# First norm with the shift as dots on VectorE and chunks handed over singly; last block finished and stored chunk by chunk

## The reference

```python
mod = silu(c) @ ada_w.T + ada_b              # (B, 6 D)
shift_msa, scale_msa, gate_msa, shift_mlp, scale_mlp, gate_mlp = split(mod, 6)
h = rmsnorm(x, g1) * (1 + scale_msa) + shift_msa
q, k, v = heads(h @ qkv_w.T + qkv_b)         # q, k normed over 36, q scaled
o = softmax(q @ k.T) @ v                     # per head
x = x + tanh(gate_msa) * (o @ proj_w.T + proj_b)
h2 = rmsnorm(x, g2) * (1 + scale_mlp) + shift_mlp
x = x + tanh(gate_mlp) * (gelu(h2 @ fc1_w.T + fc1_b) @ fc2_w.T + fc2_b)
```

## Time and profile before

| | |
|---|---|
| median of 3 runs | 2960.52 us (2960.25 to 2960.9) |
| profiled execution, its own time | 2961.68 us |
| its span | 2959.8 us |
| TensorE (PE) busy | 98% |
| VectorE (DVE) busy | 67% |
| ScalarE (ACT) busy | 53% |
| GpSimd (POOL) busy | 7% |

### The profile page before, as it was taken

The page is one execution under the profiler, slowest core; times in us unless marked ns, Lnnn a source line. Parts: engine busy times, 40 slices in busy tenths (PEclk is TensorE's granted clock), DMA queues, the critical chain, the costliest instruction groups (busy, mean ns, idle before and its releaser), DMA issues.

```text
span 2959.8 us, 35431 instructions
## 1 busy us (share of the span) xinstructions
PE 2900.7 (98%) x13080; PEld 2194.8 (74%) x13080; DVE 1971.7 (67%) x2687; ACT 1581.8 (53%) x1926; POOL 220.1 (7%) x153
## 2 busy tenths in 40 slices
PE   8999996999999999999999999999999999999998
PEld 7999994666666666666666666688888888888886
DVE  5777775899888888888888887844343342424332
ACT  3333324677676676776776766634344343434342
POOL 3232301000000000000000000090000000000000
PEclk9999997999999999999999999999999999999999
DMA  5465545222222222322223223342222222322121
GB/s 211 150 194 160 177 142 157 63 82 76 75 83 76 74 72 75 86 77 79 79 62 86 73 76 95 116 139 89 72 85 72 80 77 91 102 77 88 41 68 45
DMA packets 238407, 282.85 MB, mean 96 GB/s; under 512 B 34912, under 2 KB 143968, under 8 KB 237344
## 3 DMA queue, kind: packets, MB, share of 16 engines
q1 hardware_dynamic: 232992, 270.18, 30.0%
q10 hardware_dynamic: 5248, 10.49, 1.0%
HBM read 195.66 MB, written 84.67 MB: 95 GB/s over the span
## 4 chain that ended last, share of the span: by engine, by line
PE 82%; DVE 1%; ACT 1%; SPq 0%; DMA 0%; issue 0%; POOL 0%; DVEq 0%; ACTq 0%; POOLq 0%
PE ps L1385 16%; PE ps L1410 16%; PE ps L1469 15%; PE ps L1452 15%; PE ps L1397 13%; PE ps L1428 4%; PE ps L1396 2%; ACT gated L1092 1%; DVE x L1267 0%; SPq L874 0%; DVE x L1271 0%; DVE x L1273 0%; DVE w_lo L1261 0%; DMA kT<-qk_hi_scratch 0%; POOL kT L1007 0%
## 5 line engine op out<-in xcount | busy, mean ns | idle before, releaser
L1039 ACT ACTIVATE p_r<-ps 128x1024 f32<-128x1024 f32 x512 | 491.9, 1024 | 423.6 <-PE ps L1385 423.6
L1216 DVE TENSOR_TENSOR p_lo<-p_r,p_hi 128x1024 fp32r<-128x1024 f32 x512 | 613.2, 1218 | 0.0
L1385 PE MATMUL ps<-qT,kT 110*128 110x512 f32 x2048 | 573.6, 397 | 21.2 <-DMA qT<-m_scratch 19.8
L1385 PEld LDWEIGHTS ps<-qT,kT 110*128 110x128 f32 x2048 | 382.8, 190 | 155.4 <-issue 51.4
L1039 ACT ACTIVATE prob<-ps 128x1024 f32<-128x1024 f32 x512 | 483.5, 1030 | 2.1 <-PE ps L1385 1.6
L1396 PE MATMUL ps<-prob,vp 128*64 128x512 f32 x1024 | 453.1, 595 | 0.0
L1397 PE MATMUL ps<-prob,vp 128*37 128x512 f32 x1024 | 451.7, 594 | 0.0
L1338 DVE TENSOR_TENSOR a_lo<-act,a_hi 128x512 fp32r<-128x512 f32 x144 | 102.7, 713 | 518.9 <-ACT a_hi L1082 518.9
L1210 DVE CAST p_hi<-p_r 128x1024 fp32r<-128x1024 f32 x512 | 350.1, 694 | 135.0 <-ACT p_r L1039 133.6
L1469 PE MATMUL ps<-a_hi,w 128*128 128x512 f32 x1296 | 415.6, 393 | 0.6 <-DVE a_lo L1338 0.6
L1410 PE MATMUL ps<-p_hi,vx 128*128 128x512 f32 x1024 | 404.1, 395 | 0.1
(11 more groups left out here) (165 smaller groups left out, 3612.5 us busy)
## 6 DMA issues: line engine op xcount, KB each, us to landing
w_raw<-w SPq DMA_DIRECT2D x144, 320.0 KB, 2.9
qk_hi_scratch<-aw SPq DMA_DIRECT2D x32, 576.0 KB, 3.1
qk_lo_scratch<-aw SPq DMA_DIRECT2D x32, 576.0 KB, 4.4
kT<-qk_hi_scratch SPq DMA_DIRECT2D x128, 144.0 KB
qT<-qk_hi_scratch SPq DMA_DIRECT2D x128, 144.0 KB
v_scratch<-stv SPq DMA_DIRECT2D x32, 512.0 KB, 2.6
vp<-v_scratch SPq DMA_DIRECT2D x16, 1024.0 KB, 9.1
xb<-xT SPq DMA_DIRECT2D x8, 1280.0 KB, 10.0
```

Of the source, the lines that this page charges most:

```text
L1039: act.activation(out, ps[:, 2 * slot:2 * slot + 2, :].rearrange("p a b -> p (a b)"), ACT.Exp).then_inc(exp_done, 1)
L1216: dve.tensor_tensor(p_lo[:, j], p_r[:, j], f32(p_hi[:, q % HIGHS]), ALU.subtract).then_inc(plo_done, 1)
L1385: mm = pe.matmul(ps[:, 2 * (entry % RING) + h, :], kT[r][:, h, kt * P:(kt + 1) * P], qT[:, u % 2, h], start=True, stop=True)
```

## The change

At the start: TensorE makes the scale alone, in one group; the shift of both sequences is made by dots on VectorE (`shift`), for sequence 0 ahead of the sum of squares, for sequence 1 after the first tile's weights are ready and ahead of the tile loop. The order of the weights `ada`, `adan` follows. The maximum and the product on 128x8 elements become tensor_tensor with a small tensor that is broadcast, prepared before. VectorE makes x * scale * norm in one operation per chunk (`scaled`), ScalarE adds the shift while it makes the high part, VectorE adds it again while it makes the low part (`h0_low`), and each low part releases one chunk of TensorE's first tile. The low parts of w, pieces 1, 2 and 3, are made in halves (chunks 0 and 1, chunks 2 to 4) and awaited so. Pieces 2 and 3 of w have buffers of their own and are loaded at once.

At the end: in block 7, TensorE finishes the partial chunk first at k = 17 and signals every chunk; gates and adds follow in that order; SP stores the partial chunk, chunks 0 and 1, chunk 2 and chunk 3 as four transfers.

```diff
+        w_raw2 = sb(st, "w_raw2", [P, KC, PIECE])
+        w_raw3 = sb(st, "w_raw3", [P, KC, PIECE])
...
+        W_HALVES = (slice(0, 2), slice(2, KC))
+        W_LOWS = ((0, slice(0, KC)),) + tuple((q, ks) for q in (1, 2) for ks in W_HALVES)
@@ SP
-                for s in range(2):
-                    sp.dma_start(aw01[:, s], ada[:, s]).then_inc(aw_ld[s], 16)
+                sp.dma_start(awp, ada).then_inc(aw_ld[1], 16)
+                sp.dma_start(aws, adan[0]).then_inc(aw_ld[0], 16)
...
                 load_w(1)
+                load_w(2)
+                load_w(3)
                 sp.wait_ge(zero_done, 1)
                 sp.dma_start(m_s...)
+                sp.dma_start(xb[:, 1], xT[:, :, N:N + BLK]).then_inc(x_ld[1], 16)
+                sp.wait_ge(dot_done, KC)
+                sp.dma_start(bias[:], qkvb.partition_broadcast(P)).then_inc(bias_ld, 16)
                 sp.wait_ge(mod_mm, 1)
...
@@ GpSimd
-                for q in range(NP - 1):
+                for n, (q, ks) in enumerate(W_LOWS):
+                    cols = slice(q * PIECE, (q + 1) * PIECE)
                     pool.wait_ge(whi_done, q + 1)
+                    wait(pool, wlo_done, n)
+                    pool.tensor_tensor(w_lo[:, ks, cols], raw[q][:, ks], f32(w_hi[:, ks, cols]), ALU.subtract).then_inc(wlo_done, 1)
@@ reciprocal
-                dve.tensor_scalar(rs[:], rs[:], EPS, None, ALU.max).then_inc(r_max, 1)
+                dve.tensor_tensor(rs[:], rs[:], eps_t[:].unsqueeze(2).to_broadcast([P, TPB, 2]), ALU.max).then_inc(r_max, 1)
...
-                dve.tensor_scalar(rs[:], rs[:], float(D) ** 0.5, gain[:, 0:1], ALU.mult, ALU.mult).then_inc(r_done, 1)
+                dve.tensor_tensor(rs[:], rs[:], root_gain[:].unsqueeze(2).to_broadcast([P, TPB, 2]), ALU.mult).then_inc(r_done, 1)
@@ ScalarE
                 for m in range(KC):
-                    ...
-                    affine(act, 0, m)
                     act.wait_ge(aff_done, m + 1)
-                    act.activation(h_hi[:, 0, m], tmp[:, m], ACT.Copy).then_inc(hhi0_done, 1)
-                split_w(2)
+                    act.activation(h_hi[:, 0, m], tmp[:, m], ACT.Identity,
+                                   bias=mod[:, SHIFT_MSA, m, 0:1], scale=1.0).then_inc(hhi0_done, 1)
+                    if m == 1:
+                        split_w(2)
                 split_w(3)
-                act.wait_ge(wlo_last, 1)
+                act.wait_ge(wlo_done, 1)
@@ VectorE
+                def shift(r, product):
+                    for m in range(KC):
+                        wait(dve, dot_done, KC * r + m)
+                        dve.tensor_tensor_reduce(product, aws[:, m], c_b[:, r], 1.0, 0.0, ALU.mult, ALU.add,
+                                                 dots[:, r, m:m + 1]).then_inc(dot_done, 1)
+                    dve.wait_ge(dot_done, KC * (r + 1))
+                    dve.tensor_tensor(mod[:, SHIFT_MSA, :, r], dots[:, r], adab_t[:, 0:KC], ALU.add).then_inc(modn_add, 1)
+                dve.wait_ge(cb_done, 3)
+                dve.wait_ge(aw_ld[0], 16)
+                shift(0, bias[:, 0:D])
                 dve.wait_ge(sq0_done, KC)
                 sum_chunks(dve, 0)
...
+                reciprocal(dve, 0)
...
+                def scaled(m):
+                    dve.scalar_tensor_tensor(tmp[:, m], xb[:, 0, m], mod[:, SCALE_MSA, m, 0:1], RB, ALU.mult,
+                                             ALU.mult).then_inc(aff_done, 1)
+                def h0_low(m):
+                    dve.wait_ge(hhi0_done, m + 1)
+                    ...
+                    dve.scalar_tensor_tensor(out, tmp[part, m], mod[part, SHIFT_MSA, m, 0:1], f32(h_hi[part, 0, m]), ALU.add,
+                                             ALU.subtract).then_inc(hlo_done, 1)
+                scaled(0)
+                for m in range(1, KC):
+                    scaled(m)
+                    h0_low(m - 1)
+                dve.wait_ge(aff_done, KC)
+                h0_low(KC - 1)
+                dve.tensor_copy(warm[:], eps_t[:]).then_inc(xr_done, 1)
+                for ks in W_HALVES:
+                    ...
+                    dve.tensor_tensor(w_lo[:, ks, cols], raw[NP - 1][:, ks], f32(w_hi[:, ks, cols]), ALU.subtract).then_inc(wlo_last, 1)
...

+                dve.wait_ge(wlo_done, 1)
+                shift(1, prod)
                 dve.wait_ge(bias_ld, 16)
@@ TensorE
                         for k in range(KC):
+                            if first and r == 0 and t == 0:
+                                if h == 0:
+                                    pe.wait_ge(hlo_done, k + 1)
+                                if k in (0, W_HALVES[1].start):
+                                    pe.wait_ge(wlo_done, 2 * h + 2 + (k > 0))
+                                    if h == 1:
+                                        pe.wait_ge(wlo_last, 1 + (k > 0))
@@ the last block
+    def order_out(i):
+        return range(KC) if i < NB - 1 else (KF,) + tuple(range(KF))
...
+            for n, ms in ((1, slice(KF, KC)), (3, slice(0, 2)), (4, slice(2, 3)), (5, slice(3, 4))):
+                sp.wait_ge(out_done, KC * (NB - 1) + n)
+                sp.dma_start(outT[:, ms, columns_of(NB - 1)], x1[(NB - 1) % 2][:, ms]).then_inc(last_dma, 16)
```

More of the change, by code:

```diff
@@ L184, in qkv_phase @@
         NTILES = B * N // P
-        RB, MOD0 = ps[:, 4, :], ps[:, 5, 0:KC * B].rearrange("p (m b) -> p m b", b=B)
-        MOD1 = [ps[:, m if m < KF else 6, 0:B] for m in range(KC)]
+        W_HALVES = (slice(0, 2), slice(2, KC))
+        W_LOWS = ((0, slice(0, KC)),) + tuple((q, ks) for q in (1, 2) for ks in W_HALVES)
+        RB, MOD1 = ps[:, 4, :], ps[:, 5, 0:KC * B].rearrange("p (m b) -> p m b", b=B)
         RT = RB[:, 0:2 * TPB].rearrange("p (t c) -> p t c", c=2)
@@ L536, in _, with modulate @@
             def _(pe):
-                def modulate(s, m):
-                    out = MOD1[m] if s else MOD0[:, m]
+                def modulate(m):
                     for k in range(KC):
                         rows = slice(0, P if k < KF else TL)
-                        mm = pe.matmul(out, aw01[rows, s, k, m * P:(m + 1) * P], c_s[rows, k],
+                        mm = pe.matmul(MOD1[:, m], awp[rows, k, m * P:(m + 1) * P], c_s[rows, k],
                                        start=k == 0, stop=k == KC - 1)
@@ L596, in tile @@
                     for h in range(2):
[L597 to L601 removed]
+                        if not (first and r == 0 and t == 0):
                             pe.wait_ge(evac_done, 2 * tt + h - 1)
                         for k in range(KC):
+                            if first and r == 0 and t == 0:
[5 more added lines that the diff above has]
+                                        pe.wait_ge(wlo_last, 1 + (k > 0))
                             for n, (w, a) in enumerate(passes(k, w_hi, w_lo, h_hi, h_lo)):
@@ L618, in body @@
                         i = B * it + r
-                        pe.wait_ge(hlo_done, i + 1)
+                        if not (first and r == 0):
+                            pe.wait_ge(hlo_done, KC * (i + 1))
                         for t in range(TPB):
@@ L765, in main_phase @@
     gate_done, tail_done, out_done = sem("gate_done"), sem("tail_done"), sem("out_done")
-    out_dma = [sem(f"out_dma{j}") for j in range(2)]
+    out_dma, last_dma = [sem(f"out_dma{j}") for j in range(2)], sem("last_dma")
     OA, OBK = ps[:, 6, :], ps[:, 7, :]
@@ L1264, in add_out @@
                 out = x1[i % 2]
[L1265 to L1273 removed]
+                for n, m in enumerate(order_out(i)):
+                    dve.wait_ge(gate_done, KC * i + n + 1)
+                    if m < KF:
+                        dve.tensor_tensor(out[:, m], out[:, m], gated[:, n % 2], ALU.add).then_inc(out_done, 1)
+                    else:
+                        dve.tensor_copy(tmp[0:TL, 0], gated[TL:P, n % 2]).then_inc(tail_done, 1)
+                        dve.tensor_tensor(out[0:TL, KF], out[0:TL, KF], gated[0:TL, n % 2], ALU.add).then_inc(tail_done, 1)
+                        dve.wait_ge(tail_done, 2 * i + 2)
+                        dve.tensor_tensor(out[0:TL, KF], out[0:TL, KF], tmp[0:TL, 0], ALU.add).then_inc(out_done, 1)
             with dve.If(dve.value_load(unbounded[0:1, 0:1], min_val=0, max_val=1) > 0):
@@ L1461, in fc2 @@
                     pe.wait_ge(w2_done, 2 * k + 2)
-                for m in range(KC):
+                for m in order_out(i) if k == FC - 1 else range(KC):
                     if k == 0 and i > 0:
                         pe.wait_ge(gate_done, KC * (i - 1) + m + 1)
+                    final = j == NB * FC - 1
                     hi = w2c[:, k, D + TL + m * P:D + TL + (m + 1) * P] if m < KF else w2c[:, k, KF * P:DP]
```

137 lines of the change are left out of this document (56 added, 81 removed).

## The result

Over 20 runs of each kernel the changed one takes 2957.39 us (2955.34 to 2960.00), the kernel before 2961.97 (2959.99 to 2963.88): a ratio of 0.9985, 95% interval 0.9978 to 0.9991, or 4.6 us less. The forecast was 2957.5. Part of that closeness is luck: it was reached as 2960.5 - 3.0, and the gain is 4.6 from a start that the larger set puts at 2962.0.

A forecast was written before the change was run, and what follows sets the result against it. TensorE, busy 98% of the span, was taken as the bound, so only its waits at start and end count. Start +2.1 and end -5.1 gave -3.0 us, 2960.5 to 2957.5; range 2949 to 2961.

The forecast's parts named there:

- maximum, product end with GpSimd's instructions: First norm: both small VectorE operations wait for GpSimd's instructions; product released at 30.3 instead of 33.33, 3.0 us earlier.
- lows 2, 3, 4 end: First tile's chunks: VectorE's low parts alternate with GpSimd's halves of piece 2, ending at 39.3, 42.85 and 43.45.
- evacuation ends, tile 1 starts: After tile 0: dots alternating with GpSimd's sums delay the evacuation to 57.8; tile 1 starts at 57.85, 0.5 before 58.37.
- slow restart costs: Tile 1's start: idle TensorE's clock falls, so 16 matmuls run at 0.36 rather than 0.197, costing 2.6 us.
- start in all: Whole start: tile 1 0.5 us earlier plus 2.6 for slow matmuls, a net loss of 2.1 us.
- TensorE's end to last add: Block 7: reordered gates and single adds finish the last add at 2951.15, 2.8 us earlier than 2953.96.
- end in all: Last block: earlier adds and four stores land at 2954.2, 5.1 us less.
- the lower bound of the store: Final store: if nothing but the last 256 KB counted, landing at 2952.3; given as -6.6 us.
- (a): Rival at the first norm: small two-tensor operations do not wait; 2955.3, or 2952.7 if the clock does not fall; chance 0.15.
- (b): Rival at tile 1: as forecast, but TensorE's clock stays up through the gap; 2954.9; chance 0.17.
- (c): Rival before tile 1: sequence 1's dots hardly meet GpSimd, evacuation at 52, no slow restart; 2949.5; chance 0.16.
- (d): Rival at tile 1: restart stays at 1.2 GHz longer, slower overall; 2964 if all of tile 1 is slow; chance 0.05.

The follow-up runs named there:

- matmuls in the gap: Changed kernel plus 34 matmuls with unread results in TensorE's idle time between tile 0 and tile 1; 2955.04 us, 0.9978 of the kernel before.
- dots after the evacuations: Changed kernel with sequence 1's five dots moved behind both evacuations of tile 0; 2948.86 us, 0.9955 of the kernel before.
- small operations with a scalar: Changed kernel with the norm's maximum and product as tensor_scalar again; 2958.47 us, 0.9988 of the kernel before.
- sums later: Changed kernel with GpSimd's first sum of squares waiting for the evacuation of half 0 of tile 0; 2955.83 us, 0.9977 of the kernel before.
- one store: Changed kernel with its last block stored by one transfer of all five chunks instead of four; 2959.33 us, 0.9991 of the kernel before.
- end alone: Kernel before with only the changed last block; 2957.79 us, 0.9986 of the kernel before.
- start alone: Changed kernel with the last block of the kernel before; 2962.46 us, 1.0002 of the kernel before.

## Why the prediction was right, point by point

| step | forecast | measured |
|---|---|---|
| maximum, product end with GpSimd's instructions | 28.27, 30.3 | 28.31, 30.45 |
| tile 0 starts | 34.8 | 35.03 |
| lows 2, 3, 4 end | 39.3, 42.85, 43.45 | 39.43, 42.82, 43.60 |
| tile 0 ends | 50.4 to 53.1 | 50.60 |
| evacuation ends, tile 1 starts | 57.8, 57.85 | 57.29, 57.35 |
| slow restart costs | 2.6 | 2.6 (65.45 - 57.35 - 5.5) |
| start in all | +2.1 | +1.6 |
| TensorE's end to last add | 2.98 | 3.14 |
| end in all | -5.1 | -5.6 |

The decisive reading, that VectorE's small operations are short and wait for GpSimd, held for the two-tensor form too. The Trainium skill, page "SBUF — State Buffer", section "Who interferes with whom", says that a Vector instruction with two SBUF inputs waits for a GpSimd instruction that reads SBUF; down to 128x5 elements (1.10 us where 0.17 is its work) this case agrees. So the mechanism that ate the lead was foreseen, and so was its place. Not every operation on SBUF waits, though. The reciprocal on 128x8 elements took 0.20 at 28.68 in the kernel before, while GpSimd's 28.56 to 33.30 ran, and the product right behind it waited to the end.

Two sizes were off, in opposite directions. The evacuation ended 0.5 earlier than forecast: a step of dot and sum took 1.71 us ((55.17 - 46.63) / 5), not 1.87. The end's gain was 0.5 too small: landing was reckoned to 2959.36, while the span of before ends at 2959.8; and the median of the 256 KB stores landed 2.4 us after issue, so that the span ended 2.91 after the last add where 3.05 was forecast. A third had no effect: the modulation ended at 18.57, not 21.2, and TensorE waited for the squares anyway.

One bound does not come out of its own numbers: 2952.3 less 2959.36 is -7.1, where the lower bound of the store is given as -6.6. The measured end lies inside either.

The Trainium skill, page "VectorE: DVE Perf Modes", section "What auto-detection actually checks", speaks of outermost non-unit dimensions that are both even or equal. The forecast took this to reach operations on 128x1 elements, and by that reading the three on `bound` would have waited (+0.8). They took 0.21, 0.15 and 0.15, the last two begun 0.10 and 0.29 us after GpSimd's 46.23. So the measurement decides against that reading; one element per partition has no non-unit dimension, and the sentence does not say what holds then.

The forecast passes a shift of tile 1 on to the end in full, though TensorE idles 7.90 us before 456.57 and 19.81 us before attention. In the main this held: with matmuls in the gap the sum came 2.3 earlier and the time fell by 2.35, with the dots after the evacuations it was 8.8 and 8.5.

The rivals, each now with a price. (a) Small operations free: the trace refutes it; put into PSUM they are worth 1.9, the forecast had 2.15. (b) The clock stays up: refuted by the 0.50 from 57 to 62; worth 2.35, forecast 2.6. It leaned on one row, in which the granted clock fell 4.4 us after TensorE stopped; here TensorE stopped at 50.60 and the clock averaged 0.80 from 52 to 53 and 0.50 from 53 to 54, while in "small operations with a scalar" TensorE stopped at 52.14 and it was still 1.00 from 52 to 54. So that row's time from stop to fall is no fixed number, and how near (b) came cannot be read from it. (c) The dots meet no GpSimd: refuted. The forecast had 8.0 for it. Taking GpSimd's sums away from the dots brought only 1.6 ("sums later"), since the sums then are late themselves; moving the dots behind the evacuations, which is another change, brought 8.5. (d) A longer slow stretch: it was over at 63, 5.7 us.

What one trace tells of the start's size is less sure than the table looks. The profiled execution of the changed kernel falls back further behind 65.45, to 2.3 us at the first attention matmul (480.86 for 478.56) and 4.0 at TensorE's end (2952.15 for 2948.16). The kernel with one store has the same start, and its trace has the sum at 64.16, attention at 478.54 and TensorE's end at 2948.55, 0.4 behind the kernel before. So the fall-back belongs to single executions and not to the change, and the start's loss is 0.3 to 1.8 us by the four traces with this start (0.7 more of each if it is taken from end alone's 63.21, whose start is that of before), 0.7 by the medians of start alone. The forecast of +2.1 there is confirmed in kind, a lead given back and a slow restart, but not to the tenth. Open: why executions of one kernel differ by this much, and whether the split of w's low parts into halves helps by itself, which was not tried.

## What to carry to other kernels

An engine is made late by what stands in its queue ahead of the thing awaited: five dots that nobody needed yet cost 8.5 us in front of an evacuation, by the run that moved them behind it, and what they cost there (0.94 us of idle time) these runs do not resolve in the time. Before shortening a chain, ask what waits next and what the idle time does to TensorE's clock. And when a tiny VectorE operation shows microseconds, compare its end with GpSimd's, then change its operands' place (one in PSUM), not its form. Behind a longer wait, look also at the pace of the matmuls some microseconds after TensorE has resumed: in "sums later" the slow stretch began 2.2 us after it.

## What the runs showed of the hardware

- One-source operations on 128x1 elements did not wait beside GpSimd (0.15 us at 46.33 and 46.52, GpSimd's sum from 46.23), while tensor_scalar on 128x8 did (3.34). A reciprocal did not, neither on 128x8 (0.20) nor on 128x32: in "sums later" it took 0.35 inside GpSimd's 59.59 to 60.85, and the tensor_scalar right behind it waited to the end. With one input in PSUM the 128x8 tensor_tensor took 0.17.

```profile
59.58 0.35 DVE L497 RECIPROCAL rt<-rt 128x32 f32<-128x32 f32 x1
59.97 0.91 DVE L499 TENSOR_SCALAR rt<-rt,qscale 128x16 f32<-128x16 f32 x1
```

- After 6.75 and 5.30 us of idle time tile 1 started slow (half 0 in 8.1 and 8.2 us), after 1.40 us it did not. After 2.91 us ("sums later", at 60.91) the matmuls first ran at the full pace and were slow from 63.09 to 66.61, with a granted clock of 0.50 from 64 to 66.
- The granted clock can read 1.00 where matmuls run at the slow pace: in the kernel before it is 1.00 from 44 to 50, with pairs 0.72 apart from 44.41 on. The spacing is the safer reading; 57 to 62 us after the change shows both, 0.50 and 0.72.
- From issue to landing, stores at the end took 2.4 us for 256 KB (median of three; 2.7 in end alone), 2.7 for 512 KB, and 5.0 for 1280 KB (5.4 in the kernel before).
